# One stage in place of two between the scan and attention: convolution output and QKV projection joined

## What is computed

```python
x = x + conv(gn(x))            # selective scan in 4 directions, then:
    yc = (yc - mu) * rsqrt(var + 1e-5) * ln_weight + ln_bias   # mean, variance over 192 channels
    y  = gelu(yc)
t = tokens(x)
t = t + attention(ln(t))       # ln over the 192 channels again; 12 heads of 16; bias by relative position
    qkv = ln(t) @ qkv_w.T + qkv_b
t = t + experts(ln(t))         # 4 experts, the best 2 of each token
```

## Time and profile before

| | |
|---|---|
| median of 3 runs | 2886.11 us (2885.58 to 2888.05) |
| the profiled execution | 2886.54 us, its span 2884.5 us |
| granted TensorE clock, mean | 0.831 of 2.4 GHz |
| busy share of the span | TensorE 79%, VectorE 73%, ScalarE 46%, GpSimd 49% |
| convolution output | 1398.79 to 1447.53 us |
| QKV | 1447.53 to 1579.03 us |
| attention, first score | 1594.22 us |

### The profile page before, as it was taken

One profiled execution on the slowest core, in us unless ns is written; L12 is line 12 of the kernel. 1 busy time (PEld: TensorE's weight loads), 2 busy tenths in 40 slices (PEclk: granted clock), 3 DMA queues, 4 the chain that ended last, 5 costly groups with the idle time before them and its releaser, 6 DMA issues. The chain is left out here.

```text
span 2884.5 us, 32999 instructions
## 1 busy us (share of the span) xinstructions
PE 2266.9 (79%) x8803; PEld 801.2 (28%) x8803; DVE 2114.8 (73%) x2874; ACT 1339.7 (46%) x1866; POOL 1406.6 (49%) x714
## 2 busy tenths in 40 slices
PE   3676666666666666656576799999999879999999
PEld 1111111111111111111133123322333236766766
DVE  4999999999999999999555788787878652221212
ACT  3445444544454444445455167676767532212121
POOL 3999999999999999999721100000000020000000
PEclk9666757767776766777688599999999979999999
DMA  4544544454455444544314411321312340000000
GB/s 120 173 149 159 179 157 150 161 182 157 140 167 175 164 141 162 173 161 147 117 51 104 54 24 25 42 29 24 46 24 31 61 107 6 6 6 6 6 6 11
DMA packets 97109, 274.03 MB, mean 95 GB/s; under 512 B 16958, under 2 KB 22657, under 8 KB 96897
## 3 DMA queue, kind: packets, MB, share of 16 engines
q1 hardware_dynamic: 92858, 271.89, 33.4%
q10 hardware_dynamic: 4078, 0.19, 0.1%
HBM read 226.55 MB, written 41.22 MB: 93 GB/s over the span
## 5 line engine op out<-in xcount | busy, mean ns | idle before, releaser
L607 POOL TENSOR_TENSOR hs<-hs,c_rep 128x1024 f32<-128x1024 f32 x384 | 897.4, 2355 | 81.1 <-DVE hs L703 51.5
L451 PE MATMUL psU<-b_stack,b_sel 96*128 96x512 bf16 x640 | 310.9, 498 | 451.1 <-DVE hs L703 448.7
L1595 DVE TENSOR_REDUCE mx<-ps 128x1 f32<-128x512 f32 x864 | 539.4, 683 | 115.4 <-PE ps L1434 110.3
L1570 ACT ACTIVATE P<-ps 128x512 f32<-128x512 f32 x768 | 417.7, 599 | 247.1 <-PE ps L1446 223.0
L653 DVE TENSOR_TENSOR psU<-psU,dtu_rep 128x512 f32<-128x512 f32 x640 | 431.3, 679 | 26.8 <-DMA dtu_rep<-dt_rows 10.9
L419 PE MATMUL psY<-hs,state_sel 128*32 128x512 f32 x1572 | 425.9, 904 | 13.8 <-POOL hs L607 8.9
L547 ACT ACTIVATE decay<-dt_rep,a_neg 128x1024 f32<-128x1024 f32 x320 | 360.5, 1140 | 158.4 <-DVE hs L703 134.6
L703 DVE TENSOR_TENSOR_SCAN hs<-decay,hs,psU 128x512 f32<-128x512 f32 x320 | 408.0, 1275 | 2.3
L703 DVE TENSOR_TENSOR_SCAN hs<-decay,psU 128x512 f32<-128x512 f32 x320 | 388.2, 1213 | 0.0
L1434 PE MATMUL ps<-ks,qs 96*128 96x512 bf16 x864 | 344.7, 403 | 34.4 <-DMA ks<-qk_parts 23.8
L451 PEld LDWEIGHTS psU<-b_stack,b_sel 96*128 96x128 bf16 x640 | 62.7, 100 | 975.8 <-DVE hs L703 876.2
(11 more groups left out here) (226 smaller groups left out, 2377.5 us busy)
## 6 DMA issues: line engine op xcount, KB each, us to landing
c_rep<-bc_rows SPq DMA_DIRECT2D x132, 512.0 KB, 4.9
dt_rep<-dt_rows SPq DMA_DIRECT2D x99, 512.0 KB, 4.7
dtu_rep<-dt_rows SPq DMA_DIRECT2D x99, 512.0 KB, 6.3
b_rep<-bc_rows SPq DMA_DIRECT2D x33, 512.0 KB, 6.1
dt_rows<-dt SPq DMA_DIRECT2D x33, 384.0 KB, 3.3
dt_rows<-soft SPq DMA_DIRECT2D x33, 384.0 KB, 3.4
qs<-qk_parts SPq DMA_DIRECT2D x90, 128.0 KB, 6.6
ks<-qk_parts SPq DMA_DIRECT2D x90, 128.0 KB, 7.2
```

What stands on the lines that cost most here:

```text
L451: pe.matmul(psU[:, q % UR, :], s.b_sel[:, r, nq, :], b_stack[:, p, CH * pos:CH * pos + CH], start=True, stop=True).then_inc(b_spread, 1)
L607: pool.tensor_tensor(h, h, c_rep[:, nq, :], ALU.mult).then_inc(hc_ready, 1)
L1570: nc.scalar.activation(P[:, kt % 2, head, :], ps2[:, bank, :], ACT.Exp).then_inc(exp_done, 1)
L1595: v.reduce_max(mx[:, slot, u:u + 1], ps1[:, (slot * MAXES + u) % R, :], AX.X).then_inc(max_done, 1)
```

## The change

`conv_out` and `qkv` become one block, `mid`. The norm that belongs to the convolution (kind 0, in place in `s.Y`) and that ahead of QKV (kind 1, into a ring `Z` of two images) share one sequence of norm steps, numbered by `FIRST`, with one set of semaphores, one `ps_mean`, one `ps_var` and a ring `work` of four slots. The input is loaded again image by image into a ring of two, and GELU and its addition run image by image. Image b's projections stand beside the kind 1 steps of image b + 1 and the kind 0 steps of image b + 2.

The first four norm steps, (0,0), (0,1), (1,0), (1,1), don't use GpSimd: TensorE multiplies both channel halves (and both halves of the squares) by the averaging matrix and sums them in PSUM.

Q and K channels are projected 128 at a time rather than 96, so the loop has 24 steps (6 an image) of 128 channels by 512 tokens. `parts` has four slots of 512 columns; bias and scale are columns `qb` and `scl` over 128 partitions. The low part moves from VectorE to GpSimd (`low_part`). `w_proj`, the bias and the corner tables are made ahead of the loop or in its first steps, their DMAs issued at steps 6 and 7. `qs` and `ks` live outside attention now, and SyncE loads image 0's stacks at steps 8 to 16 of the loop. `s.V` holds 16 columns a head; `v_now` is cleared and gets its ones in attention. The copy of the bias table to DRAM moves to `prepare`. `qk_parts` is laid out by 384 joint channels.

```diff
-def conv_out(nc, w, s):
-def qkv(nc, w, s):
+def mid(nc, w, s):
+        SLOTS, RING, VRING, NORMS = 4, 4, 2, 4
+        DIRECT = 4
+        V_OF = ((0, 1), (2,), (3,), (4, 5), (6,), (7,))
+        FIRST = {(0, 0): 0, (0, 1): 1, (1, 0): 2, (1, 1): 3, (0, 2): 4, (0, 3): 5}
+        for b in range(NB - 1):
+            for kind, ahead in ((0, 2), (1, 1)):
+                for c in range(2):
+                    if b + ahead < NB:
+                        FIRST[kind, 2 * (b + ahead) + c] = len(FIRST)
+        def norm_steps(b, x, first, second):
+            if b == 0 and x < 2:
+                second(0, 2 + x)
+            if b + 2 < NB:
+                if x < 2:
+                    first(0, 2 * (b + 2) + x)
+                if x in (2, 3):
+                    second(0, 2 * (b + 2) + x - 2)
+            if b + 1 < NB:
+                if x in (3, 4):
+                    first(1, 2 * (b + 1) + x - 3)
+                if x in (4, 5):
+                    second(1, 2 * (b + 1) + x - 4)
+        def gelu_at(b, x):
+            return b + 1 < NB and x == (0 if b else 1)
...
+            # sync
+                for i in range(NQ):
+                    if x == 5 and b + 2 < NB:
+                        sp.wait_ge(x_added, 2 * (b + 1))
+                        load_x(b + 2)
+                    sp.wait_ge(lo_ready, i + 1)
+                    sp.dma_start(s.qk_dram[b, :, 128 * m:128 * m + 128, CH * c:CH * c + CH]...)
+                    at = i - (GROUPS + 2)
+                    if 0 <= at < 9:
+                        for j in (2 * (at % 3), 2 * (at % 3) + 1):
+                            load_stack(at // 3, j)
...
+            # gpsimd
+                def low_part(i):
+                    pool.wait_ge(mid_ready, i + 1)
+                    pool.tensor_tensor(parts[:, i % SLOTS, 2, :], rest[:, i % SLOTS, :], parts[:, i % SLOTS, 1, :],
+                                       ALU.subtract).then_inc(lo_ready, 1)
+                for b in range(NB):
+                    for x in range(GROUPS):
+                        if b + 2 < NB:
+                            if x < 2:
+                                add_halves(0, 2 * (b + 2) + x)
+                            if x in (1, 2):
+                                add_squares(0, 2 * (b + 2) + x - 1)
+                        if i:
+                            low_part(i - 1)
+                        if b + 1 < NB:
+                            if x in (4, 5):
+                                add_squares(1, 2 * (b + 1) + x - 4)
+                            if x in (3, 4):
+                                add_halves(1, 2 * (b + 1) + x - 3)
...
+            # tensor
+                def mean(kind, c):
+                    if n < DIRECT:
+                        for f in range(2):
+                            m = pe.matmul(ps_mean[:, :], s.average[:], half(s.Y, c, NB)[:, f, :], start=(f == 0), stop=(f == 1))
...
+                mean(0, 0)
+                mean(0, 1)
+                # weight transposes
+                variance(0, 0)
+                variance(0, 1)
+                # output weights, bias and corners turned
+                mean(1, 0)
+                mean(1, 1)
+                variance(1, 0)
+                mean(0, 2)
+                variance(1, 1)
+                mean(0, 3)
+                for b, x:   # one projection, its V projections, norm_steps(b, x, mean, variance)
...
+            # scalar, step i
+                    nc.scalar.activation(val[:, i % SLOTS, :], ps_w[:, i % RING, :], ACT.Identity,
+                                         bias=qb[:, m:m + 1], scale=scl[:, m:m + 1])
+                    nc.scalar.copy(parts[:, i % SLOTS, 0, :], val[:, i % SLOTS, :])
+                    if i:
+                        middle_part(i - 1)
+                    norm_steps(b, x, square, invert)
+                    if gelu_at(b, x):
+                        gelu(b + 1)      # table load, two GELUs, table load
...
+            # vector, step i
+                    # V additions of V_OF[x], rest of step i
+                    if x and gelu_at(b, x - 1):
+                        add_x(b + 1)
+                    norm_steps(b, x, centre, scale)
+                    # at i == 2: split the corners in three parts
```

More of the change, by code:

```diff
@@ L996, in qkv @@
[L996 to L1002, removed]
@@ L1036, in _ @@
[L1036 to L1042, removed]
@@ L1069, in _ @@
                                        pattern=[[-1, 128]], channel_multiplier=1).then_inc(pool_ready, 1)
[L1070 to L1076, removed]
+                add_halves(0, 2)
@@ L1078, in _ @@
+                low_part(NQ - 1)
             @block.tensor
             def _(pe):
[L1080 to L1090, removed]
@@ new lines, in variance @@
+                def variance(kind, c):
+                    n = FIRST[kind, c]
+                    if n:
+                        pe.wait_ge(log_ready, n)
+                    if n < DIRECT:
+                        pe.wait_ge(squared, n + 1)
+                        for f in range(2):
+                            m = pe.matmul(ps_var[:, :], s.average[:], work[:, n % NORMS, f, :], start=(f == 0), stop=(f == 1))
+                        m.then_inc(var_ready, 1)
+                        return
+                    pe.wait_ge(sq_ready, n - DIRECT + 1)
+                    pe.matmul(ps_var[:, :], s.average[:], work[:, n % NORMS, 0, :], start=True, stop=True).then_inc(var_ready, 1)
@@ new lines, in middle_part @@
+                def middle_part(i):
+                    act.wait_ge(rest_ready, i + 1)
+                    nc.scalar.copy(parts[:, i % SLOTS, 1, :], rest[:, i % SLOTS, :]).then_inc(mid_ready, 1)
+                nc.scalar.preload_act_table_set("natural_log_exp_and_others")
+                square(0, 0)
+                square(0, 1)
+                invert(0, 0)
+                invert(0, 1)
+                gelu(0)
+                square(1, 0)
+                square(1, 1)
+                invert(1, 0)
@@ new lines, in centre, with scale @@
+                def centre(kind, c):
+                    n = FIRST[kind, c]
+                    v.wait_ge(mean_ready, n + 1)
+                    if kind and c >= 4:
+                        v.wait_ge(v_proj, 8 * (c // 2 - 1))
+                        v.wait_ge(q_proj, GROUPS * (c // 2 - 1))
+                    v.tensor_tensor(norm_out(kind, c), half(s.Y, c, NB), ps_mean[:, :].unsqueeze(1).broadcast_to([HC, 2, CH]),
+                                    ALU.subtract).then_inc(centred, 1)
+                def scale(kind, c):
+                    n = FIRST[kind, c]
+                    v.wait_ge(dev_ready, n + 1)
+                    v.wait_ge(centred, n + 1)
+                    z = norm_out(kind, c)
+                    v.tensor_tensor(z, z, work[:, n % NORMS, 1, :].unsqueeze(1).broadcast_to([HC, 2, CH]), ALU.mult
+                                    ).then_inc(normed, 1)
@@ new lines, in add_x @@
+                def add_x(b):
+                    v.wait_ge(x_in[b % 2], 16 * (b // 2 + 1))
+                    for f in range(2):
+                        v.wait_ge(gelu_done, 2 * b + f + 1)
+                        v.tensor_tensor(s.Y[:, b, f, :], raw[:, b % 2, f, :], s.Y[:, b, f, :], ALU.add).then_inc(x_added, 1)
+                centre(0, 0)
+                centre(0, 1)
+                v.memset(scl[:, 0:1], DH ** -0.5)
+                v.memset(scl[0:64, 1:2], DH ** -0.5)
+                v.memset(scl[64:128, 1:2], 1.0)
@@ L1231, in _ @@
                 t.then_inc(padded, 1)
+                scale(0, 0)
+                scale(0, 1)
+                v.wait_ge(w_turned, 1)
+                for f in range(2):
+                    for g in range(2):
+                        t = v.tensor_copy(w_qkv[:, f, 3 * HC * g:3 * HC * g + 3 * HC], ps_w[0:HC, 2 * f + g, 0:3 * HC])
+                t.then_inc(w_taken, 1)
                 v.wait_ge(tab_in, 16)
@@ L1241, in _ @@
[L1241 removed]
+                own(v.tensor_copy(corners[:, 1, :, :].rearrange("p h j -> p (h j)"), ps_w[0:19, RING - 1, 0:19 * HEADS]))
                 own.wait()
[L1243 to L1251 removed]
@@ L1295, in attention @@
         psM = ctx.enter_context(nc.psum_tensor("psM", [128, CH], F32))
-        stack_in = [sem(f"stack_in{i}") for i in range(NHG)]
         rows_set = sem("rows_set")
@@ L1403, in maxima @@
                     sp.wait_ge(nm_in, (i + 1) * 16)
-                for hg in range(NHG):
-                    load(0, hg)
                 sp.wait_ge(misc_taken, 1)
```

400 lines of the change are left out of this document (207 added, 193 removed).

## The result

The joined stage makes the kernel slower: 2915.07 us median of 4 runs (2910.34 to 2919.43) against 2887.08 of the kernel before (4 runs, 2885.58 to 2888.48), a ratio of 1.0097 (95% interval 1.0079 to 1.0115). That is 28 us more; forecast were 13 (2899), with a range up to 2914, so the measured median lies 1 us above that range. The profiled execution took 2910.34 us.

The account below looks back on a forecast made before the run. TensorE was taken to bound the middle of the old stage, dependent short steps both sides, and queue waits the new loop. Fill -28.9, loop +64 and border -21.6 gave +13.5, so 2899 us, range 2880 to 2914.

Parts of the forecast that it names:

- fill: From the stage's start to its first projection: 36 us where it was 64.9, gain 28.9, bounds 36.1 and 21.3.
- loop: From first projection to the last store's landing: 172 us where it was 108, loss 64, bounds 51.5 and 93.
- border: From the last store's landing to attention's first score: about 0.9 us left, gain 21.6, or 6.4 without earlier loads.
- nothing after it: Behind attention's first score: instructions are kept, so a shift of that start shifts the end by the same amount.
- the pair of 3.15 us: VectorE scale pieces took 3.15 us beside a GpSimd addition of 1.26, 1.28 without: one waits out the other.
- the walk: Each queue of the loop taken in program order with earlier prices: 159.5 us at 2.4 GHz, 201.3 at 1.2 GHz.
- The direction: The whole kernel gets slower: 2899 us against 2886.1, chance of slower 0.64.
- its three distances: In the loop, the images follow each other 55, 50 and 43 us apart.
- the GpSimd queue as what holds the means: In the loop, means wait for GpSimd's halves, which stand in its queue behind those for middle parts.
- Rival 1: The clock stays high and the joined loop wins: 2880 us, just faster; chance 0.14.
- Rivals 3 and 4: Loads hold back stores in the loop, some 10 us, 2909; early loads do not shorten the border, 2914; 0.06 each.
- Rival 2: The loop's queues interlock less than counted, 1 us a step in 18 steps: 2881 us; chance 0.14.

Follow-up runs that it names:

- after_pad24: The kernel after with nothing but 24 one-column memsets added on VectorE at the stage's end: 2909.9 us, 1.0074 of the kernel before.
- border_undone: The kernel after with image 0's operand loads issued at attention's start again, not at steps 8 to 16 of the loop: 2934.0 us, 1.0137 of the kernel before.
- pool_order: The kernel after with halves and kind 1 squares ahead of the previous step's low part in GpSimd's queue: 2881.5 us, 0.9952 of the kernel before.
- low_direct: The kernel after with the low part on VectorE and TensorE's direct sums in all 16 norm steps: 2869.5 us, 0.9930 of the kernel before.
- pool_pad24: The kernel after with GpSimd's queue reordered and 24 one-column memsets on VectorE at the stage's end: 2872.0 us, 0.9937 of the kernel before.

## Why the forecast was wrong

**The sum.** Forecast: fill -28.9, loop +64, border -21.6, nothing after it. Measured: the fill 38.4 instead of 36 (-26.5), first projection to the last store's landing near 1610.4, 175.6 instead of 172 (+67.6), border 1.05 instead of 0.9 (-21.5), and +6.6 after it: 26.2 from the stage's start on, in the profiled executions, 28 in the medians. The spans of the two profiled executions differ by 23.8 only, since in this one the stage began 2.4 us sooner. The 2 us between 26.2 and 28 are within what the start of the stage does by itself: it stood between 1396.2 and 1404.7 us in the thirteen profiles of kernels with the joined stage.

**The step that failed** is the sentence "What follows is set by the attention and expert stages, which keep their instructions; from the first score on VectorE reduces scores back to back, so a shift of that start shifts the end by the same amount." The instructions stayed, their place in VectorE's program did not. The time behind the first score grew by 6.6 us, and 5.9 of these are the place: `after_pad24` takes them back on this very kernel, with nothing else changed. The other 0.7 stay open. Without it the median would have been near 2908.5, inside the range. I had put this term at nothing, with no bound. The row in the trace of before that could have warned me is the 2.35 us of VectorE's "issue" at an edge: an idle time without a releaser where a loop turns belongs to the turn and not to the instructions, and the change was going to move the code.

**Terms that were off in size.** The fill by 2.4 us: I took the middle of the two clock levels, 36, and the measured 38.4 stands two thirds of the way from 28.8 to 43.6, at a granted clock of 0.71; one microsecond of it is the corner select on GpSimd, 2.56 us long where I had next to nothing, for which TensorE's queue waited. The loop by 3.6 us: GpSimd's sums of the halves took 1.50 us on the mean (1.26 in my sum, 12 of them) and the additions of x 1.70 (1.15, 8 of them). Both run beside the other engine of the pair whose pieces wait each other out; how much of the 3.6 either explains no run separates. And the earlier trace rows was read too short: between the start and the end of the pair of 3.15 us (1413.95 to 1417.10) there stood a second GpSimd addition beside the one at 1413.59, in the kernel before:

```profile
1415.29 1.26 POOL L911 TENSOR_TENSOR lc_sq<-lc_sq 96x512 f32<-96x512 f32 x1 [0.44 <-ACT lc_sq L886]
```

So the 1.9 us lost stand against two additions, not one. That the loop came within 4 us is in part luck: the walk itself gave 159.5 and 201.3 for the two clock levels, and the 172 between them rests on a guess of the clock, 0.75, which turned out at 0.78.

**What was right.** The direction, the loop as the loss, its three distances within 1.6 us each, the border's gain and the GpSimd queue as what holds the means. Rival 1 (the clock stays high) did not come about, at 0.78 in the loop. Rivals 3 and 4 are out, both by `border_undone`. Rival 2, looser queues, is what the kernel after didn't have and `pool_order` has: 35 us, from the order of one queue.

**What the change is worth.** Joined with an order that doesn't interlock, it wins: `low_direct` took 2869.46 us (4 runs, 2866.43 to 2875.94), 0.9930 (0.9910 to 0.9951) of the kernel before, `pool_pad24` 2871.98 with the low part still on GpSimd.

## What to carry to other kernels

When work moves onto an in-order queue, look at what stands behind it: a piece that waits late in the chain must stand behind those whose inputs are ready early, even if it belongs to an older step. A walk through the queues in program order, with durations from the rows of before and a guess of the clock, came within 4 us of this loop's 175.6; for another order of one queue I expected 25 to 35 us less, and 35.1 were measured. And a change that adds or drops instructions ahead of a loop that branches at run time (`Fori`) moves that loop's code: where an engine idles by "issue" at each turn of it, give this a term of some microseconds with either sign, and try a few small paddings before judging the edit.

## What the runs showed of the hardware

The length of a loop's turn depended on the position of its code: 24 extra VectorE instructions of 0.38 us together made the whole kernel 5.9 us faster, and 256 left the long edges as they were. The long turn holds one packet more of the instruction queue q14, at some 2.3 us. With more work on TensorE and GpSimd's sums gone, the granted clock in the loop was 0.90 instead of 0.78, while the stage got 36 us shorter. The scan, unchanged, ended up to 8.5 us apart from one execution to another.
